# Storing the parts of q and k in five pieces as they are made, in a fused attention and mixture-of-experts layer

## The reference

```
mod = silu(c) @ wmod                       # six rows per batch: shifts, scales, gates
h = layernorm(x) * (1 + ca) + sa
q, gate, k, v = h @ Wq, h @ Wk, h @ Wv (+ biases)      # 16 heads of 8 features
q, k = rmsnorm(q) * qn_w, rmsnorm(k) * kn_w            # per head
attn = softmax(q k^T / sqrt(8)) v, times sigmoid(gate)
x = x + ga * (attn @ Wo + bo)
h = layernorm(x) * (1 + cb) + sb
x = x + gb * (sum over the top 2 of 32 experts of weight * h @ W_expert)
```

## Time and profile before

| what | value |
|---|---|
| runs, us | 898.12, 899.68, 902.56 (median 899.68) |
| the profiled execution, us | 901.62, span of its instructions 899.9 |
| busy in the span | PE 713.3, DVE 679.2, ACT 561.3, POOL 512.5 us |
| mean granted TensorE clock | 0.921 of full |
| DMA | 141.70 MB in all, 157 GB/s on average |
| packets of SyncE's and ScalarE's queue q1 | 99.54 MB, 44.4% of 16 engines' span |

### The profile page before, as it was taken

The page is one execution under the profiler, slowest core; times in us unless marked ns, Lnnn a source line. Parts: engine busy times, 40 slices in busy tenths (PEclk is TensorE's granted clock), DMA queues, the critical chain, the costliest instruction groups (busy, mean ns, idle before and its releaser), DMA issues.

```text
span 899.9 us, 23375 instructions
## 1 busy us (share of the span) xinstructions
PE 713.3 (79%) x6334; PEld 495.5 (55%) x6334; DVE 679.2 (75%) x2015; ACT 561.3 (62%) x1300; POOL 512.5 (57%) x846
## 2 busy tenths in 40 slices
PE   4479888989988899999889898888988743633865
PEld 1245555556545566666666666565665543633765
DVE  4768788989878888889988889999997345403666
ACT  2247777878776788888778787777777624412100
POOL 5212256666665566666556777777776764335442
PEclk8579999999999999999999999999999965857988
DMA  5435565556655677777667778776675545747422
GB/s 160 101 90 135 137 165 130 128 126 162 149 138 127 164 186 186 192 190 191 178 163 187 187 198 197 188 189 178 178 191 148 148 133 157 217 126 195 130 67 87
DMA packets 178001, 141.70 MB, mean 157 GB/s; under 512 B 19540, under 2 KB 162612, under 8 KB 177876
## 3 DMA queue, kind: packets, MB, share of 16 engines
q1 hardware_dynamic: 122804, 99.54, 44.4%
q10 hardware_dynamic: 47392, 24.92, 9.8%
q0 software_dynamic: 7680, 15.74, 6.2%
HBM read 81.77 MB, written 57.80 MB: 155 GB/s over the span
## 4 chain that ended last, share of the span: by engine, by line
PE 33%; DVE 16%; issue 15%; DMA 11%; SPq 10%; POOL 6%; another core or an unknown queue 5%; ACT 3%; POOLq 0%; DVEq 0%; ACTq 0%
PE mx_ps L1942 8%; PE o_ps L1991 6%; PE st_ps L1977 6%; DVE negmax L1402 5%; DMA k_aug<-k_d 4%; SPq L650 3%; DMA k_d<-parts 2%; PE misc L1915 2%; DMA mod_o<-mod_d 2%; PE st_ps L2141 2%; SPq L602 2%; PE misc L2000 2%; POOL parts L797 1%; SPq L626 1%
## 5 line engine op out<-in xcount | busy, mean ns | idle before, releaser
L1402 DVE TENSOR_REDUCE negmax<-mx_ps 128x2 f32<-128x512 f32 x512 | 338.3, 686 | 63.1 <-PE mx_ps L1942 55.4
L1094 ACT ACTIVATE pr<-st_ps 128x512 f32<-128x512 f32 x512 | 286.4, 600 | 47.6 <-PE st_ps L1977 45.7
L1942 PE MATMUL mx_ps<-k_aug,q_aug 126*128 126x256 bf16 x1024 | 192.2, 279 | 52.0 <-DMA k_aug<-k_d 24.0
L1977 PE MATMUL st_ps<-q_aug,k_aug 128*128 128x256 bf16 x1024 | 180.9, 274 | 1.7 <-issue 1.2
L924 POOL DMA_INDIRECT yg<-ys_d,gidx x120 | 118.2, 985 | 89.0 <-DVE yb L1632 39.9
L1942 PEld LDWEIGHTS mx_ps<-k_aug,q_aug 126*128 126x128 bf16 x1024 | 82.7, 99 | 136.1 <-issue 125.9
L1991 PE MATMUL o_ps<-pr,v_aug 128*32 128x256 f32 x2048 | 140.0, 391 | 20.4 <-issue 13.3
L909 POOL DMA_INDIRECT xs_d<-h,slot x120 | 121.7, 1014 | 47.1 <-DVE slot L1505 24.4
L1977 PEld LDWEIGHTS st_ps<-q_aug,k_aug 128*128 128x128 bf16 x1024 | 97.5, 100 | 26.2 <-issue 10.2
L1991 PEld LDWEIGHTS o_ps<-pr,v_aug 128*32 128x32 f32 x2048 | 55.8, 110 | 70.2 <-issue 49.8
L1100 ACT ACTIVATE oT<-o_ps 128x256 f32<-128x256 f32 x128 | 49.0, 383 | 51.0 <-PE o_ps L1991 29.4
(11 more groups left out here) (192 smaller groups left out, 1295.8 us busy)
## 6 DMA issues: line engine op xcount, KB each, us to landing
xs_sb<-xs_d SPq DMA_DIRECT2D x248, 64.0 KB
ys_d<-ys_sb ACTq DMA_DIRECT2D x62, 256.0 KB
q_aug<-q_d SPq DMA_DIRECT2D x64, 192.0 KB
mod_o<-mod_d SPq DMA_DIRECT2D x32, 256.0 KB
bias_p<-bias_d SPq DMA_DIRECT2D x32, 200.0 KB
q_d<-parts SPq DMA_DIRECT2D x32, 192.0 KB
k_d<-parts SPq DMA_DIRECT2D x32, 192.0 KB
k_aug<-k_d SPq DMA_DIRECT2D x64, 96.0 KB
```

The source lines that it names most:

```text
L1094: nc.scalar.activation(pr[:, h % PR], st_ps[score_bank(b, h)][:], ACT.Exp, scale=SCALE).then_inc(exp_d, 1)
L1402: v.tensor_reduce(negmax[:, :, h], mx_ps[h % 2][:], AX.X, ALU.max, negate=True).then_inc(mx_d, 1)
L1942: last = t_.matmul(mx_ps[h % 2][:, qc], q_aug[b.par][0:MROW, h, qc * P:(qc + 1) * P], k_aug[b.par][0:MROW, h, :], start=True, stop=True)
L1977: last = t_.matmul(st_ps[score_bank(b, h)][:, kc], k_aug[b.par][:, h, kc * P:(kc + 1) * P], q_aug[b.par][:, h, :], start=True, stop=True)
```

## The change

The four stores become five, each issued as soon as its parts are there: behind `hi_d` the high q rows; behind `mid_d` the middle q rows and, in one store of 128 KB, the high and middle k parts; behind `lo_d` the low q rows and the low k part (64 KB each). The counts at which others wait for the stores go from 64 to 80 per batch. Nothing else is changed.

```diff
+PARTS = 5
...
             def store_parts(b):
-                wait(sp, lo_d, b.n + 1)
+                def rows_of_q(a):
+                    row, n = sum(TERMS[:a]), TERMS[a]
+                    sp.dma_start(q_d[b.par, row:row + n].rearrange("a p t -> p a t"),
+                                 parts[:, 0, a:a + 1, :].broadcast_to([P, n, NT])).then_inc(parts_st, 16)
+
+                def rows_of_k(a, n):
+                    sp.dma_start(k_d[b.par, a:a + n].rearrange("a p t -> p a t"), parts[:, 1, a:a + n]).then_inc(parts_st, 16)
+
+                wait(sp, hi_d, 2 * (b.n + 1))
                 sp.nop(nofuse=True)
                 for half in range(2):
                     wait(sp, aug_ld[b.par][half], 64 * b.nth)
                 sp.nop(nofuse=True)
-                row = 0
-                for a, n in enumerate(TERMS):
-                    sp.dma_start(q_d[b.par, row:row + n].rearrange("a p t -> p a t"),
-                                 parts[:, 0, a:a + 1, :].broadcast_to([P, n, NT])).then_inc(parts_st, 16)
-                    row += n
-                sp.dma_start(k_d[b.par].rearrange("a p t -> p a t"), parts[:, 1]).then_inc(parts_st, 16)
+                rows_of_q(0)
+                wait(sp, mid_d, b.n + 1)
+                sp.nop(nofuse=True)
+                rows_of_q(1)
+                rows_of_k(0, 2)
+                wait(sp, lo_d, b.n + 1)
+                sp.nop(nofuse=True)
+                rows_of_q(2)
+                rows_of_k(2, 1)
...
             def load_heads(b, j):
...
-                wait(sp, parts_st, 64 * (b.n + 1))
+                wait(sp, parts_st, PARTS * 16 * (b.n + 1))
...
             def low_part(b):
                 wait(gp, mid_d, b.n + 1)
-                wait(gp, parts_st, 64 * b.n)
+                wait(gp, parts_st, PARTS * 16 * b.n)
...
             def high_part(b):
...
-                wait(act, parts_st, 64 * b.n)
+                wait(act, parts_st, PARTS * 16 * b.n)
...
             def middle_part(b):
                 wait(act, rest_d, b.n + 1)
-                wait(act, parts_st, 64 * b.n)
+                wait(act, parts_st, PARTS * 16 * b.n)
```

## The result

The changed kernel takes 884.87 us (median of 4 runs, 881.22 to 887.27) beside 900.40 us of the kernel before (4 runs, 898.12 to 902.56): ratio 0.9861, 95% interval 0.9819 to 0.9903. So the change is worth 11 to 13 us by the ratios (the two intervals together reach from 6.5 to 16 us); the plain medians are 15 us apart in both cases. The profiled execution took 885.02 us with a span of 883.3.

The account below looks back on a forecast made before the run. The bound was a chain through SyncE's stores and loads to PE's first scores and VectorE's first maxima. 0.97 + 5.9 + 1.3 + 1.5 = 9.7 us off gave a median of 890.0 us, range 882 to 897.5.

Parts of the forecast that it names:

- Which chain, and where it pays: Parts, stores, landing, loads, first scores and maxima set the step in seven batches up to 14; late two thirds gain nothing.
- 5.9 + 1.3 in the sum: Gains in us: 5.9 from earlier loads in seven steps, 1.3 from long issues and late landings moved off the low part.
- the second kind: Steps where PE still has older work at the first scores: an earlier load gives nothing, VectorE's 1.0 to 1.4 us idle stays.
- Behind the low part, the issues: SyncE's four issues of 1.95 us behind the low-part wait become two of 0.98 us, ending 0.97 us earlier.
- The landing: Wait from the last store's issue to the loads, left at 1.73 us; 2.25 and up to 3.6 were seen.
- The fifth store: Adds 32 issues of 0.46 us, hidden under SyncE's wait; without that cover loads are 0.5 us later; nothing counted.
- rival D: SyncE reaches the stores only after the low part, so five issues stand there: +0.5 us in seven steps, 903; chance 0.04.
- Start-up: Batch 0's first maximum gains the whole 0.97 us; batch 1 gains nothing.
- The clock: Shorter PE pauses save two of four falls of the granted clock at 0.75 us each, 1.5 us.
- Rival A: The wait moves to PE's older work, all steps become the second kind: 2.9 us gained, 897; chance 0.18.
- Rival B: Clock falls and long issues go whole, waits vanish to their caps: 15.8 us gained, 884; chance 0.17.
- C: Rival: long SyncE issues hit the last two stores and delay the loads: slower, 905 to 916 us; chance 0.06.

Follow-up runs that it names:

- early_last16: The change made in batches 16 to 31 alone, the others storing as the kernel before: 896.11 us, ratio 0.9979 to the kernel before.
- k_whole: Changed kernel with four stores: high and middle q early, low q and all of k (192 KB) behind the low part; 884.67 us, ratio 0.9858 to the kernel before.
- split_late: Changed kernel with all five stores issued behind the low parts: 901.15 us, ratio 1.0048 to the kernel before.
- heads_first: Changed kernel with batch 1's head loads issued ahead of the load of batch 0's rows of maxima: 813.50 us on chip C, ratio 0.9742 to the kernel before.
- order_alone: Kernel before with only batch 1's head loads moved ahead of the load of batch 0's rows of maxima: 900.15 us, ratio 0.9977.
- k_whole_order: k_whole plus batch 1's head loads ahead of the load of batch 0's rows of maxima: 885.98 us, ratio 0.9810 to the kernel before.
- clock_fill: Kernel before with five float32 matmuls keeping PE busy ahead of the load waits in batches 3, 6, 8 and 12: 834.03 us on chip C, ratio 0.9994.

## Why the prediction was right, and where a term was off

The forecast was 890.0 us, 9.7 less; measured are 11 to 13 us by the ratios, inside the range. That the number came so near is partly luck: the start and the clock gave about 5 us more on chip A's profiles than was forecast, and 2.2 us that had no term were lost elsewhere (the account below).

*Which chain, and where it pays: right.* The waits fell in the batches named, 2, 3, 6, 8, 10, 12 and 14. Idle ahead of the first maxima of batches 2 to 15 fell from 19.9 to 13.6 us, 6.3 us beside 5.9 + 1.3 in the sum. A part of it came back: in the step from batch 2 to 3 the 2.48 us of idle are gone, but the step is only 1.2 us shorter, since 1.02 us now stand at head 8 of batch 2. The loads of the second half were looked at nowhere in the prediction. What is left is the second kind, about 1.0 to 1.4 us a batch. The later batches give little or nothing: early_last16 has 0.9979.

*Behind the low part, the issues: right.* Two issues from 135.24 to 136.06 are 0.82 us, where 0.98 were reckoned. The batch named as the sign, 4, was the exception: 3.38 us from low part to loads for 2.85 forecast, because of the long issue. *The landing: mis-sized.* It was left at 1.73 us, with "Less than 1.73 can't be shown from a row". The last store is now 64 KB and lands after 1.25 us. So the loads begin 1.68 us sooner in undisturbed batches (3.82 to 2.14) and 1.36 by the medians (3.90 to 2.54), not 0.97. k_whole, with the same time, says that this half microsecond is worth too little to be told.

*The fifth store: right.* It goes under SyncE's wait; only in batches 14 and 22 do four or all five stores stand behind the low part, as in rival D. split_late shows what it costs without that cover: 4 us, 0.13 us a batch on average. *The Trainium skill's rule on batching* (DMA: Bandwidth & Descriptors, section Bandwidth; its figures are of loads that GpSimd issues) holds here only in that form: more stores on the chain cost, more stores ahead of it do not.

*Start-up: mis-sized.* 0.97 us forecast. The first maximum of batch 0 starts at 32.05 to 32.98 us in the six profiles (delays left out) in which batch 0 stores early, and at 33.97 to 35.03 in the six in which it does not: 1.9 us on average. The loads begin 2.40 us behind batch 0's low part in place of 3.77, which is 1.37; the rest, half a microsecond, lies between the loads' issue and PE's first scores (4.4 us on average, for 4.9), and its cause is open. For batch 1 nothing was forecast, and the way from batch 0 to batch 2 stayed 39.0 us on chip A (39.60 to 38.34 on D). That the load of the rows of maxima holds batch 1 up is shown by heads_first, order_alone and k_whole_order, where b0-2 is 33.9 to 34.4 us.

*The clock: mis-sized.* Two of four falls were to be saved, and all four were. The steps behind batches 3, 6, 8 and 12, without the idle at their end, took 18.08, 19.04, 19.45 and 21.49 us before and 17.68, 17.80, 18.00 and 20.05 after: 4.5 us, where 1.5 stood in the sum. That this is the clock is shown by order_alone, which stores as before and has nearly the same times at full clock (4.3 us less), and by the two profiles of the kernel before at batch 14. clock_fill could not show it. How many falls an execution has is partly chance: from 60 to 300 us the five profiles of chips A, B and D that store late in these batches have 4, 4, 3, 2 and none, the five that store early have one in all. So on average fewer than four falls are saved, about 2.4, an estimated 3 us rather than 4.5. The Trainium skill's TensorE: Matmul & The Clock Gate, section HAM oscillation, fits the first profile's rows, in which each fall follows a pause for a load; order_alone's pauses without a fall say that such a pause alone does not bring it.

*Rival A* was right about what takes over: with the loads early, each step became of the second kind, and batch 6 reads like batch 5 did. It was wrong on the price: the steps of 19 to 20 us between first maxima held pauses and low clock of their own, and came down to 19.0 to 19.3 from batch 5 to batch 12. *Rival B* (884) is the nearer to the plain median of 884.87, the forecast to the ratios (0.9861 and 0.9877 of 899.7 are 887 and 889). *C and D* are out for all but single batches: of the issues of stores up to batch 15 three take over 1.1 us, where four did, and one of them, in batch 14, stands wholly behind the low part.

The account closes on chip A's two profiles, which are 11.7 us apart at batch 15's first maximum: 3.0 us at the start (0.8 of it because the low part itself came sooner in that execution), 6.3 of idle and 4.5 of clock, less 0.9 in the first two steps and 1.3 in the step from batch 2 to 3, and 0.1 for the rest.

## What to carry to other kernels

Where a result goes through DRAM to another engine, count what stands behind its last part, issues and landing of the last store, and send the rest while the last part is being made; the same split behind the last part is a loss. Measure the room that a load has with a delay put ahead of it, not from the distance of two records: the engine's records can run ahead of its work. When one load comes sooner, look at what its engine waits for next, here the second half of the same heads. And look at the first steps of a pipeline by themselves, since an order that is right in the steady state can hold up one step by 5 us.

## What the runs showed of the hardware that was not expected

**Two kinds of chip.** The same program takes 897 to 904 us on chips A, B and D and 836 on C. Each chip was used once, so it is not shown whether the chip or its state at the time makes the difference. The drain is 168.5 to 170.5 us on C and 217.9 to 224.5 on the others, with the same matmuls; the mean granted clock in it is 0.88 (heads_first) beside 0.80 (first profile). On A, B and D the transposes ahead of the first scores (L2025) raise their semaphore 1.7 us after the start of their record (median over the batches; 0.29 in batch 0); on C it is 0.29 us. The view of waits shows it as waits released by "remote". The kernel before on chip D, then heads_first on chip C:

```profile
PE mx_ps L1942 <- DMA k_aug<-k_d: 28.2, 15, 6.2
...
ACT oT L1100 <- remote: 22.5, 19, 2.1
...
DVE table L1550 <- remote: 15.9, 1, 15.9
```

```profile
PE mx_ps L1953 <- DMA k_aug<-k_d: 15.0, 19, 1.8
...
ACT oT L1111 <- PE o_ps L2002: 12.2, 28, 2.7
```

The 22.5 us of "remote" at the copies of the output and the single wait of 15.9 us in the drain are missing on C (no such line in its view), and VectorE's idle ahead of the first maxima of batches 2 to 15 is 1.5 us in heads_first, where it is 13.5 to 14.6 on the others with early stores. So the idle time of the second kind of step goes with this lag. What holds PE's work back on three chips at one place of each step stays open; the granted clock is full there in both.

**The landing by size.** Where nothing holds it up, a last store of 64 KB has landed 1.25 us after the end of its issue (behind 64 KB or 512 KB), one of 192 KB after 1.73 (behind 384 KB or 64). **Late landings** of 2.3 to 3.6 us come back in every second batch from 6 to 12, with four stores or five; their cause was not tried.
